# A deformable-convolution kernel on one core: the second copy of x taken from SBUF instead of HBM, and two loads moved back

## The reference

```python
# block 1: a 3x3 depthwise convolution, then three 32x32 channel mixes
x = x + L0(_gn(x))          # dw conv; softmax(att); pointwise; softmax(glob)
# block 2: offsets from a 3x3 convolution, bilinear sampling, a 3x3 convolution
def _deform(x, w_off):
    off = _conv(x, w_off, 1).reshape(B * C, H * W, 2)
    rows, cols = clip(off + grid)                 # per pixel of each plane
    # four neighbours, mixed with the fractional parts of rows and cols
    return mapped
x = x + _conv(_deform(_gn(x), w_off), w_conv, 1) + b_conv
```

## Time and profile before

| what | value |
|---|---|
| median of 3 runs | 717.24 us (716.29 to 727.23) |
| the profiled execution's own time | 718.9 us |
| its span, first to last instruction | 717.1 us |
| TensorE (PE) busy | 684.6 us, 95% of the span |
| VectorE (DVE), GpSimd (POOL), ScalarE (ACT) busy | 522.7, 478.1 and 467.9 us |
| DMA, all queues | 115.64 MB, 161 GB/s on the mean |
| mean granted TensorE clock | 0.99 |

### The profile page before, as it was taken

How to read it: one execution, slowest core, us unless ns; L and a number is a source line. 1 busy time by engine, 2 the same in 40 slices (tenths; PEclk the granted TensorE clock), 3 DMA queues, 4 the chain that set the end, 5 groups by cost and what they waited for, 6 DMA issues and landing times.

```text
span 717.1 us, 10746 instructions
## 1 busy us (share of the span) xinstructions
PE 684.6 (95%) x3500; PEld 244.4 (34%) x3500; DVE 522.7 (73%) x1033; ACT 467.9 (65%) x812; POOL 478.1 (67%) x414
## 2 busy tenths in 40 slices
PE   4799979999999799999999999999999999999985
PEld 4333333333333233333333333333333333333322
DVE  3687988779956568677876589657984685578882
ACT  7587776686667365677556755576656775577870
POOL 5004867888597656866867765887658668788770
PEclk9999999999999899999999999999999999999998
DMA  8958926889557998799949896598947625477556
GB/s 142 187 111 144 143 57 158 179 178 196 126 141 165 189 213 204 171 209 189 203 112 233 173 209 152 138 236 171 225 112 177 154 66 139 114 170 178 123 118 147
DMA packets 140189, 115.64 MB, mean 161 GB/s; under 512 B 15168, under 2 KB 114016, under 8 KB 140128
## 3 DMA queue, kind: packets, MB, share of 16 engines
q1 hardware_dynamic: 116096, 103.12, 68.6%
q10 hardware_dynamic: 24032, 11.78, 9.2%
HBM read 31.59 MB, written 16.78 MB: 67 GB/s over the span
## 4 chain that ended last, share of the span: by engine, by line
PE 55%; SPq 5%; DVE 5%; ACT 3%; POOL 3%; issue 2%; DMA 1%; DVEq 0%; POOLq 0%; ACTq 0%
PE off_ps L794 27%; PE c_ps L683 24%; PE c_ps L694 2%; PE c_ps L698 2%; SPq L476 2%; SPq L395 1%; DVE other_row L1436 1%; SPq L427 1%; ACT other_row L988 1%; DMA x1b<-x1a 1%; ACT off_abs L1001 1%; DVE x1a L1421 1%; POOL row_diff L1213 1%; ACT down_ps L999 1%; POOL row_diff L1215 1%
## 5 line engine op out<-in xcount | busy, mean ns | idle before, releaser
L1436 DVE COPY_PREDICATED other_row<-down_ps,row_diff 128x768 f32<-128x768 int32 x128 | 124.7, 1028 | 124.2 <-ACT down_ps L999 124.0
L794 PE MATMUL off_ps<-x1a,wo 128*64 128x512 f32 x768 | 179.4, 601 | 4.3 <-DMA x1b<-x1a 3.7
L794 PE MATMUL off_ps<-x1b,wo 128*64 128x512 f32 x768 | 176.4, 592 | 0.0
L683 PE MATMUL c_ps<-xb,w 128*64 128x512 f32 x336 | 149.6, 593 | 2.2 <-DVE x1a L1421 1.6
L683 PE MATMUL c_ps<-mapb,w 128*64 128x512 f32 x336 | 150.8, 594 | 0.5 <-ACT bias L977 0.3
L685 PE MATMUL c_ps<-xa,w 128*64 128x512 f32 x336 | 149.6, 593 | 0.0
L988 ACT ACTIVATE other_row<-row_diff 128x768 f32<-128x768 f32 x128 | 100.7, 835 | 66.4 <-POOL row_diff L1215 43.8
L1230 POOL TENSOR_TENSOR other_row<-other_row,x_strips 128x512 f32<-128x512 f32 x48 | 57.2, 1191 | 119.1 <-DVE other_row L1448 119.0
L685 PE MATMUL c_ps<-mapa,w 128*64 128x512 f32 x294 | 131.7, 594 | 0.0
L999 ACT ACTIVATE down_ps<-off_ps,bias_o 128x512 f32<-128x512 f32 x64 | 42.0, 656 | 106.8 <-PE off_ps L794 99.4
L1231 POOL TENSOR_TENSOR other_col<-other_col,other_row 128x512 f32<-128x512 f32 x64 | 86.3, 1349 | 31.3 <-DVE other_row L1448 31.3
(11 more groups left out here) (135 smaller groups left out, 978.5 us busy)
## 6 DMA issues: line engine op xcount, KB each, us to landing
mapa<-mapped SPq DMA_DIRECT2D x224, 65.0 KB, 2.0
x1b<-x1a SPq DMA_DIRECT2D x28, 520.0 KB, 6.5
mapb<-mapa SPq DMA_DIRECT2D x28, 520.0 KB, 7.6
out_dram<-x1a SPq DMA_DIRECT2D x49, 256.0 KB, 4.7
xb<-in_x_dram SPq DMA_DIRECT2D x48, 256.0 KB, 9.9
xa<-in_x_dram ACTq DMA_DIRECT2D x40, 256.0 KB, 8.7
x_strips<-x1a SPq DMA_DIRECT2D x112, 81.2 KB, 2.5
x_strips<-x1a SPq DMA_DIRECT2D x112, 65.0 KB, 2.5
```

The lines of the kernel that those rows point to most:

```text
L683: nc.tensor.matmul(bank[0:64, :], weights[:, kx, :], rows_b[:, of, kx:kx + W], start=(kx == 0), stop=(kx == 2))
L794: last = nc.tensor.matmul(off_ps[k % 2][64 * t:64 * t + 64, CH * n:CH * n + CH], wo[wpar][:, kx, side:side + 2 * C], rows[:, b:b + 7:2, kx ...
L1436: last = dve.copy_predicated(other_row[n][:, :, KR // 2 * odd:KR // 2 * odd + KR // 2, :], bass.AP(tensor=rows.tensor, offset=rows.offset ...
```

## The change

`xb` of an image isn't read from HBM any more. Once a half of `xa` has landed, SP copies it within SBUF, in two DMAs of 64 partitions with 8,320 bytes each (16 blocks of 130 columns, 520 KB in all). Image 0's `xb` is made by ACT as before. In turns from 1 on, the copy of half 0 stands where both loads stood, and that of half 1 behind the strips of half 0. The exception for turn 2 goes: ACT's loads of `xa` for image 4 stand behind chunks 1 and 3, and DVE's statistics of it behind chunks 4 and 5.

```diff
@@ constants @@
-    LATE_LOADS = 2
-    XA_LOADS_BEHIND = [3, 4]
     def stats_chunks(i):
-        return [1, 2, 3] if i == 0 else [5, 6, 6] if i == LATE_LOADS else [4, 5, 5]
+        return [1, 2, 3] if i == 0 else [4, 5, 5]
@@ block.sync @@
-            def load_xb(i, half, loaded):
-                rows = x[i].rearrange("c (b r) w -> c b r w", r=4)
-                to = xb_of(i)
-                b, e = half * HB, half * HB + HB
-                for q in range(4):
-                    first = b + 1 if q < 2 else b
-                    sp.dma_start(to[Q * q:Q * q + Q, first:first + HB, 1:W + 1], rows[:, b:e, (q + 2) % 4, :])\
-                      .then_inc(loaded[half], DMA)
+            def copy_xb(i, half, copied):
+                to, rows = xb_of(i), xa_of(i)
+                b, e = half * HB, half * HB + HB
+                for first, p, p_from in ((b + 1, 0, 2 * Q), (b, 2 * Q, 0)):
+                    sp.dma_start(to[p:p + 2 * Q, first:first + HB, :].rearrange("p b w -> p (b w)"),
+                                 rows[p_from:p_from + 2 * Q, b:e, :].rearrange("p b w -> p (b w)"))\
+                      .then_inc(copied[half], DMA)
...
             sp.wait_ge(cleared, 1)
             for half in range(2):
-                load_xb(1, half, ahead_xb_loaded)
+                sp.wait_ge(ahead_loaded[half], LOADS * DMA)
+                copy_xb(1, half, ahead_xb_copied)
...
                 for half in range(2):
-                    load_xb(2, half, xb_loaded)
+                    sp.wait_ge(xa_loaded[half], xa_count(2))
+                    copy_xb(2, half, xb_copied)
...
                 if after and prev:
-                    for half in range(2):
-                        sp.wait_ge(conv1_done, 8 * (i + 1) + (5 if half == 0 else 8))
-                        load_xb(i + 2, half, xb_loaded)
+                    sp.wait_ge(conv1_done, 8 * (i + 1) + 5)
+                    sp.wait_ge(xa_loaded[0], xa_count(i + 2))
+                    copy_xb(i + 2, 0, xb_copied)
...
                     sp.wait_ge(mapped_ready, NK * i + 4)
-                    for half in range(2 if i >= 2 else 1):
-                        move_strips(sp, i + 1, half)
+                    move_strips(sp, i + 1, 0)
+                    if prev and after:
+                        sp.wait_ge(conv1_done, 8 * (i + 1) + 8)
+                        sp.wait_ge(xa_loaded[1], xa_count(i + 2))
+                        copy_xb(i + 2, 1, xb_copied)
+                    if i >= 2:
+                        move_strips(sp, i + 1, 1)
@@ block.scalar, pad_x and the turns @@
-                            act.wait_ge(xb_loaded[half], LOADS * DMA * (i - 1))
+                            act.wait_ge(xb_copied[half], COPIES * DMA * (i - 1))
...
-                        if prev and i + 2 < NB and (k == XA_LOADS_BEHIND[half] if i == LATE_LOADS
-                                                    else 4 * half + 3 in groups):
+                        if prev and i + 2 < NB and 4 * half + 3 in groups:
                             act.wait_ge(conv1_done, 8 * (i + 1) + 4 * half + 4)
                             load_x(act, i + 2, half, xa_loaded)
```

More of the change, by code:

```diff
@@ L251, in deformable_preact_kernel @@
         ahead_loaded = [sem(f"x_ahead_loaded{n}") for n in range(2)]
-        ahead_xb_loaded = [sem(f"x_ahead_xb_loaded{n}") for n in range(2)]
+        ahead_xb_copied = [sem(f"x_ahead_xb_copied{n}") for n in range(2)]
         x1b_written = sem("x1b_written")
         xb_written = sem("xb_written")
-        xb_loaded = [sem(f"xb_loaded{n}") for n in range(2)]
+        xb_copied = [sem(f"xb_copied{n}") for n in range(2)]
         x1b_copied = [sem(f"x1b_copied{n}") for n in range(2)]
@@ L621, in _ @@
                     for half in range(2):
-                        load_xb(b, half, xb_loaded)
+                        wait_apart(xa_loaded[half], xa_count(v))
+                        copy_xb(b, half, xb_copied)
                     wait_apart(x1_pads, v + 1)
@@ L885, in pad_x @@
                         if isinstance(i, int) and i == 1:
-                            act.wait_ge(ahead_xb_loaded[half], LOADS * DMA)
+                            act.wait_ge(ahead_xb_copied[half], COPIES * DMA)
                         else:
-                            act.wait_ge(xb_loaded[half], LOADS * DMA * (i - 1))
+                            act.wait_ge(xb_copied[half], COPIES * DMA * (i - 1))
                 rows_a, rows_b, mean = xa_of(i), xb_of(i), mean_x[par]
```

## The result

The kernel before took 722.24 us at the median of four runs beside it (716.29 to 728.07), the changed one 732.42 us (729.67 to 733.51). Two of the four runs before (727.23 and 728.07 us) are in a slower state, over 1.5% above the fastest, and the ratio of 1.0213 (interval 1.0159 to 1.0266) leaves them out. So the change makes it slower, by 11 to 19 us, and its median lies outside the predicted range (711.5 to 727.0 us). Beside the experiments the kernel before had medians of 718.2 to 719.4 us, and against those the loss is 13 to 14 us. The profiled execution is the fastest of the four: 729.67 us by its own count, with a span of 727.8 us, 10.7 more than before. The trace therefore shows a somewhat smaller loss than the medians.

A forecast was written before the change was run, and what follows sets the result against it. TensorE (PE), working 684.6 of 717.1 us, was taken as the bound. Stops of +2.6 us (turns 3 and 5) and 0 (turn 2) on the profiled 718.9 us gave 721.5 us; range 711.5 to 727 us.

The forecast's parts named there:

- SP's stretch grows by 5.8 us: SP's list from x1's pads to the last mapb copy: 4.5 for the held copy plus 1.3 for strips.
- "From the pads of x1 to the last copy of `mapb`" is all that counts: Turns 2 to 5: SP's delay counts only in this stretch; time freed where the loads stood is worth nothing.
- ACT is late at chunk 1 and catches up by chunk 3: ACT's first drain waits for a store 5.8 us later; PE needs that bank only for the fourth group; no cost.
- Landing 6.7 us: The last mapb copy of a turn lands 6.7 us after SP issues it; used for PE's margins.
- Each half of `xa` has landed before SP comes to copy it: At SP's copies from xa to xb: the source is there already, so SP's list isn't held; no cost.
- Stops of 1.1 us in turn 3 and 1.5 in turn 5, 2.6 together: PE waits for mapb at its first conv2 matmul, as the 5.8 us delay exceeds margins of 4.7 and 4.3.
- turn 4, taken as turn 3 with a margin of 4.7 us: PE's slack for mapb in turn 4 starts at 4.7 us, grows to 5.8 after turn 3's stop; no stop.
- The argument that a stop helps the next turn: Turns 3 to 6: a stop moves PE back against SP's chain; margins become 5.8 in turn 4, 7.3 in turn 6.
- Turn 2 unchanged: PE's stop of 3.7 us on x1b before offset chunk 4 stays; net change 0 us.
- the 1.7 us by which SP was to be early: Turn 2: SP reaches its stores at 198.2 us instead of 199.9, then gives the gain back to ACT's moved loads.
- the clock falls at the new stops: First conv2 group of turns 3 to 5: stops cost 6.6 us each, +13 to +20, 730 to 737 us; chance 0.12.
- ACT's moved loads hold SP in turn 2: Turn 2: DMA engines alternate queues, SP 4.8 us late, x1b stop 8.5 us; 724.6 us in all; chance 0.08.

The follow-up runs named there:

- e13: The changed kernel with ACT's loads of half 1 of xa, in turns 1 to 5, issued behind its pads of x1; 723.91 us, ratio 1.0069.
- e11: The changed kernel with the store of half 0, in turns 1 to 5, issued by ACT instead of SP; 727.03 us, ratio 1.0093.
- e2: The kernel before, xb still loaded from HBM, with only ACT's loads for image 4 moved behind chunks 1 and 3; 725.65 us, ratio 1.011.
- e4: The kernel before with 13 DMAs of 128 bytes added on SP where the copy of half 1 would stand, turns 1 to 5; 765.33 us, ratio 1.0659.
- e8: The changed kernel with the store of half 0 issued by ACT and 11 DMAs of 128 bytes on SP in its place; 755.54 us, ratio 1.0512.
- e6: The kernel before with the store of half 0, in turns 1 to 5, issued by ACT instead of SP; 718.23 us, ratio 0.9998.

## Why the prediction was wrong

The step that failed: the prediction let the pads of x1 follow PE's chunks whatever SP does, so a later SP would cost its own 5.8 us and nothing more. In the runs a later SP made ACT late, and the pads with it.

- *SP's stretch grows by 5.8 us* (4.5 for the copy, 1.3 for strips without a backlog): right, 5.9 us in turn 3, 5.6 in turn 4 and 4.5 in turn 5.
- *"From the pads of x1 to the last copy of `mapb`" is all that counts; behind the old loads SP waits for ACT's pads, which follow PE's chunks*: this is the step that failed, a term put at 0 us. The pads follow PE only as long as ACT isn't held. They came 2.6 to 3.7 us later behind PE in turns 3 to 5, since ACT took 5.7 to 6.8 us instead of 2.0 to 2.7 to issue its loads beside SP's copies. With only that undone (e13), the pads are back at 9.8 us and 1.4% of the 2.1% is gone.
- *ACT is late at chunk 1 and catches up by chunk 3; costed at nothing*: wrong. ACT's wait for the store in turn 4 was 10.8 us, not 1.8 + 5.8. The store on ACT, which takes this wait away and shortens SP's list too, is worth about 1.2% (this isn't to be added to the 1.4%). What the wait costs by itself isn't shown, apart from PE's stops on ACT's x1a, 2.5 us, which are gone in e11.
- *Landing 6.7 us*: 8.3 us in turn 4, 1.6 more, where the last copy of `mapb` met ACT's loads; up to 11.3 in the experiments.
- *Each half of `xa` has landed before SP comes to copy it*: right from turn 1 on. SP's waits for loads at these copies, 9.1 us in three, are all before 130 us.
- *Stops of 1.1 us in turn 3 and 1.5 in turn 5, 2.6 together*: by the prediction's count, the copy for PE's turns 3, 4, 5 and 6 came to stops of 0.3, 3.5, 0 and 0.6 us (the fourth, 0.7 us, is in turn 2). The sign, the place and the row were right, though turn 4, taken as turn 3 with a margin of 4.7 us, had 5.3. The argument that a stop helps the next turn held too (turn 5 had none on `mapb`). But the longest was over twice the longest foreseen, and it cost 1.6 us of clock besides; two stops for ACT's x1a, 2.5 us, were not foreseen at all.
- *Turn 2 unchanged*: nearly. The second `x1b` copy was issued at 239.2 us, 2.5 later than before and beyond the 235.0 to 237.0 of the text; of this 0.95 is PE's own delay from the start. The stop grew by 1.8. The pads of image 2's x1 came at 170.6, not 169.1, and strips took 14.3 us, not 13.2. So the 1.7 us by which SP was to be early were not there, and ACT's moved loads took what the text allowed them: at the copy of `mapb` SP was 1.0 us later than before (216.5 and 215.5 us), at the copy of `x1b` behind it 2.5 (start us, us, line, DMA, count):

```profile
170.57 0.62 SPq L465 DMA_DIRECT2D x1b<-x1a  x1
...
171.89 14.28 SPq L393 DMA_DIRECT2D x_strips<-x1a  x16
...
239.15 0.64 SPq L466 DMA_DIRECT2D x1b<-x1a  x1
```

- *Rival "the clock falls at the new stops", 730 to 737 us*: this is what happened in the time, with one stop and not two or three. It named "ACT's loads, shifted against SP" as a way, though by a late landing of `mapa` and not by holding ACT. The text dismissed it with "ACT drains late by the same cause, so its loads shift along". They don't: in turn 4 ACT's second group of loads started 0.2 us behind chunk 4 as before, and SP's copy had come to it. The 0.12 was too low: in e2 SP's delay of some 2 us in turn 3 grew to a stop of 3.2 us with the lower clock in turn 5, where the text had asked for a delay of 8.
- *Rival "ACT's moved loads hold SP in turn 2"*: SP lost 1.5 us between the two copies named above, not 4.8. The larger price was paid by ACT, held in turns 3 to 5. No trace here shows whether packets by turns are the reason.

Not settled: how much of the remaining 0.7% in e13 is each of store and strips; what ACT's wait for the store costs without SP's longer list; how the loss divides between the moved loads (1.1% alone) and the copies; and why copies within SBUF hold another queue's issues more than loads from HBM do.

## What to carry to other kernels

When a queue gets later, look not only at who waits for its last transfer but at what its transfers will now run beside: an engine that issues DMAs in its own stream can stand still while it issues them (ACT 6.1 us here in place of 1.95), and its compute behind the issue is late. Busy DMA engines alone didn't do it here; it came beside copies within SBUF on another queue. A wait that is short and constant from turn to turn (9.80 us here) is a phase (one engine follows another at a fixed distance). When an edit moves it, look for a loop between the two. Replacing a load by a copy of a tile adds a dependency on that tile's landing, and so takes away the freedom to put it into the slack.

## What the runs showed of the hardware

- Four loads of 256 KB from HBM took ACT 1.95 to 2.7 us to issue beside SP's loads of `xb` from HBM (turns 3 to 5 before) and 5.7 to 6.8 us beside SP's copies of `mapb` and `xb` within SBUF (the same turns after). Each half is copied by two DMAs of 520 KB each, not by 520 KB in all as the part on the change has it.
- With 128-byte DMAs, an issue on SP took 0.63 to 0.71 us on the mean (8.19 to 9.18 for 13, e4) and up to 0.87 (9.60 for 11, e8), so a small DMA isn't a cheap way to add a little time.
- Strips beside a copy are held about alike whether their own queue or ACT's carries it (turn 3: 28.6 us with the copy's own 1.2, and 28.4, against 23.1).
- HBM read fell from 31.59 to 16.91 MB and the kernel was 2.1% slower. Whether the 0.9% of the kept copies comes from less HBM traffic or from SP's issue time, no run separates.
- At the stop of 3.5 us the granted clock was at its lower level from 427.6 to 431.1 us, at that of 5.5 us from 243.3 to 250.2, the beginning of it inside the stop. At stops of up to 1.6 us it didn't fall. At one of 2.3 us it did (e6, 244.9 to 248.3 us), so 3.7 us, the smallest that the prediction knew, isn't the smallest that costs clock.
